# A four-layer graph network on one core: each group's aggregates turned behind the next group's first gather and scattered behind its second

## The reference, cut to what matters

```python
vdeg = jnp.maximum(H_pruned.sum(axis=1), EPS)
edeg = jnp.maximum(H_pruned.sum(axis=0), EPS)
dv_isqrt = 1.0 / jnp.sqrt(vdeg)
de_inv = 1.0 / edeg
transformed = x_final @ W
agg = H_pruned.T * dv_isqrt[None, :] @ transformed
agg = agg * de_inv[:, None]
msg = dv_isqrt[:, None] * (H_pruned @ agg)
msg = msg @ Theta
return jax.nn.relu(msg)
```

## Time and profile before

| | us |
|---|---|
| median of the three timed runs | 2352.01 (2350.14 to 2352.56) |
| the profiled execution's own device time | 2343.1 |
| its span, first to last instruction | 2341.3 |
| PE busy in it | 2045.4 (87%) |
| DVE busy | 1727.1 (74%) |
| ACT busy | 754.1 (32%) |
| mean granted TensorE clock | 0.944 |

### The profile page before, as it was taken

One profiled execution on the slowest core, in us unless ns is written; L12 is line 12 of the kernel. 1 busy time (PEld: TensorE's weight loads), 2 busy tenths in 40 slices (PEclk: granted clock), 3 DMA queues, 4 the chain that ended last, 5 costly groups with the idle time before them and its releaser, 6 DMA issues. The chain is left out here.

```text
span 2341.3 us, 35832 instructions
## 1 busy us (share of the span) xinstructions
PE 2045.4 (87%) x15658; PEld 721.4 (31%) x15658; DVE 1727.1 (74%) x2056; ACT 754.1 (32%) x869; POOL 4.5 (0%) x18
## 2 busy tenths in 40 slices
PE   7998998899977777799999989987777689997997
PEld 2233333223221211233444323221111134333333
DVE  5998923288889999855541358879999965555998
ACT  0000000076634433201110036644344311112897
POOL 0000000000000000000000000000000000000000
PEclk9999999999988888799999999998888889998999
DMA  9984999899659999977789989929999987776994
GB/s 372 421 342 183 411 429 427 370 406 373 249 220 402 428 430 430 401 262 270 265 312 406 428 369 382 375 89 370 424 429 431 425 325 269 273 288 239 350 418 180
DMA packets 128043, 812.13 MB, mean 347 GB/s; under 512 B 8336, under 2 KB 10384, under 8 KB 76432
## 3 DMA queue, kind: packets, MB, share of 16 engines
q1 hardware_dynamic: 125840, 808.51, 85.9%
q10 hardware_dynamic: 2048, 1.35, 0.2%
HBM read 673.52 MB, written 136.31 MB: 346 GB/s over the span
## 5 line engine op out<-in xcount | busy, mean ns | idle before, releaser
L1215 ACT ACTIVATE stream<-stream,negmax 128x4096 f32<-128x4096 f32 x128 | 475.1, 3711 | 482.3 <-DVE negmax L1210 482.3
L1170 PE MATMUL ps<-edgeT,node_twice 64*128 64x512 f32 x1024 | 283.1, 673 | 156.8 <-DVE mx L1205 156.7
L1205 DVE CUSTOM_DVE_ANT_0 stream<-ps,stream 128x1024 f32<-128x1024 f32 x280 | 330.5, 1219 | 30.5 <-PE ps L1170 26.5
L1170 PE MATMUL ps<-edgeT,query_twice 64*128 64x512 f32 x1024 | 248.1, 616 | 4.3 <-DVE mx L1205 2.7
L579 PE MATMUL ps<-stream,moved_block 128*64 128x512 f32 x960 | 216.6, 600 | 23.6 <-DMA stream<-in_adj 23.6
L1716 PE MATMUL ps<-stream,xw 32*64 32x512 f32 x4096 | 226.5, 589 | 1.8 <-issue 1.2
L1170 PEld LDWEIGHTS ps<-edgeT,node_twice 64*128 64x128 f32 x1024 | 94.3, 201 | 343.2 <-DVE mx L1205 242.3
L1188 PE MATMUL ps<-stream,ones 128*1 128x512 f32 x1024 | 173.3, 811 | 9.4 <-DVE stream L1760 9.4
L1249 ACT ACTIVATE query_twice<-ps,less_one_exponent 128x512 int32<-128x512 int32 x256 | 154.9, 688 | 14.8 <-PE ps L1339 12.4
L1832 DVE STREAM_TRANSPOSE stream<-spare 128x4096 f32<-128x4096 f32 x22 | 97.5, 4433 | 72.5 <-PE ps L1716 51.8
L1800 ACT COPY moved_block<-ps 128x512 f32<-128x512 f32 x16 | 9.4, 586 | 408.2 <-PE ps L1688 408.2
(11 more groups left out here) (233 smaller groups left out, 1961.5 us busy)
## 6 DMA issues: line engine op xcount, KB each, us to landing
stream<-in_adj SPq DMA_DIRECT2D x118, 2048.0 KB, 16.9
pruned<-stream SPq DMA_DIRECT2D x64, 2048.0 KB, 14.7
stream<-in_adjT SPq DMA_DIRECT2D x63, 2048.0 KB, 12.0
moved_block<-in_adj SPq DMA_DIRECT2D x24, 2048.0 KB, 13.4
spare<-pruned SPq DMA_DIRECT2D x22, 2048.0 KB, 11.5
query_twice<-pruned SPq DMA_DIRECT2D x22, 2048.0 KB, 11.5
node_twice<-pruned SPq DMA_DIRECT2D x20, 2048.0 KB, 11.2
spare<-in_adj SPq DMA_DIRECT2D x18, 2048.0 KB, 9.7
```

What stands on the lines that cost most here:

```text
L1170: last = nc.tensor.matmul(ps[:, 2 * slot + h, :], stationary[F * h:F * h + F, rows_n], bank_of(edgeT[F * h:F * h + F, :], c), start=True, ...
L1205: nc.vector.tensor_tensor_reduce(out=out[:, cols], in0=ps[:, 2 * slot:2 * slot + 2, :].rearrange("p a b -> p (a b)"), in1=block_in[:, cols ...
L1215: nc.scalar.activation(out, out, ACT.Exp, bias=negmax[:, s:s + 1], accum_out=zsum[:, s:s + 1]).then_inc(exp_done, 1)
```

## The change

It moves two calls in PE's order. aggregate(g-1), which stood at the end of group g-1, now stands behind gather(4g); scatter(g-1), which stood behind gather(4g), now stands behind gather(4g+1). aggregate(7) and scatter(7) stay at the end. No instruction, wait or buffer is added or taken away, and the programs of the other engines stay as they are.

```diff
                 for g in range(groups):
                     for c in range(CH):
                         gather(CH * g + c)
                         if c == 0 and g > 0:
+                            aggregate(g - 1)
+                        if c == 1 and g > 0:
                             scatter(g - 1)
                     if g == 0:
                         pe.wait_ge(inverse_ready, 1)
...
                         last.then_inc(copies_ready, 1)
-                    aggregate(g)
+                aggregate(groups - 1)
                 scatter(groups - 1)
```

## The result

The changed kernel takes 2357.09 us (median of 11 runs, 2352.63 to 2360.15) against 2349.81 us before (11 runs, 2347.07 to 2352.56): a ratio of 1.0026, 95% interval 1.0018 to 1.0035. It is slower, by 6 to 7 us (the two medians are 7.3 apart, the ratio comes from all runs and gives 6.1); the forecast was slower by 12.5.

A forecast was written before the change was run, and what follows sets the result against it. PE sets the period before; after, a ring through turn and load binds. Per pass, start +4.6 or +4.5, ring +5.1, end -3.4, together +12.5 us on the 2352.01 median: 2364.5 us, range 2353.8 to 2371.6.

The forecast's parts named there:

- the ring: From scatter's end through turn, load and gather to the next scatter's end: 31.48 us per period, +0.85, +5.1 per pass.
- What bounds the kernel, and what hides it: PE sets the 30.63 us period; its only wait is for ACT's copy; load 12 is only 0.3 us ahead.
- The copy's wait: Aggregate waits for ACT's copy of gathered sums, some 0.8 us per group; a gather now covers it in seven of eight.
- The start: Up to the end of scatter(0), gather(4) and gather(5) now come first: +4.6 us in the first pass, +4.5 in the second.
- The end: Between scatter(6) and scatter(7) one gather less stands: 10.07 us instead of 13.51, a gain of 3.4 us per pass.
- Sum and base: Passes of +6.3 and +6.2 us give +12.5, passed on in full; on the timed median 2352.01 that is 2364.5.
- The load in time: Rival: the load behind a scatter is there 7.5 us after issue; -6.2 us in all, 2345.8; 6% to a gain.
- The clock: Rival: PE's clock falls at each wait in the ring, 1.75 us more for each of 14 gathers, 2389 us; 6%.

The follow-up runs named there:

- the doubled turn: DVE turns the third chunk of each group twice: 2349.37 us in the order before, 2441.63 us in the changed order, single runs.
- the split: Turn of chunk 4g+2 and load of chunk 4g+5 cut into halves: changed order 2343.25 us, ratio 0.9968; order before 2350.25 us, 1.0000.
- late loads: In the second pass the last layer's loads wait for the last scatter to end: order before 2348.69 us, changed order 2355.38 us.

## Why the prediction was half right

The mechanism was right and the size wrong. The step that failed is the term of the ring, +5.1 us for the six periods of each pass: it measured +2.3 and +3.5. Everything else in the sum came within about 1.5 us.

- **What bounds the kernel, and what hides it.** Right. PE's only wait in a period was the copy's, and the load was 0.3 us behind it in cover. The run with aggregate alone shows how little that cover was: 2.2 us of wait for the load instead of 0.7 for the copy.
- **The copy's wait costs 0.7 per period, and covering it is worth nothing in the ring.** Right: with it (scatter alone moved) 1.0027, without it 1.0025.
- **The ring: period 31.48, up 0.85, +5.1 per pass.** Right in kind, shown by the doubled turn and by the split; too large in size. In the three profiles it was 31.27 on average, and before it was not 30.63 but 30.89 in the first pass and 30.68 in the second. Two things made the term too large. The sum took DVE's start behind the issue, 9.09, and added 0.12 until PE starts; over the twelve loads of the first profile after, PE started 9.04 behind the issue (8.86 to 9.17), so the sum had 0.17 too much in each period, 2.0 us in all. And the other side of the difference was one clean period times six, where the row of the first to the last scatter would have given 185.3 and 183.9 for six: the pauses of PE inside scatters, in the trace of before for anyone who adds up the periods, cost before 1.9 us in the two passes, and in the changed kernel they don't show, for a reason that stays open. 10.2 us were forecast for the two middles. The shorter ring takes 2.5 off (12 x 0.21, of which the 2.0), the pauses of before 1.9, and 5.8 are left.
- **The start, +4.6 and +4.5.** Right in the second pass (+4.4). In the first, +4.5 from gather(2) on in the first pair of profiles; the table's 5.5 holds also that gather(0) stands differently to load 2 from run to run.
- **The end, -3.4 each.** Right up to the start of the last scatter, which stands 13.5 us behind the end of the one before it in every profile of before and 10.1 in every one of the changed kernel, and right with late loads (3.4). The table differs by what the last scatter loses. In the first pass it is 14.3 to 15.2 us long in the changed kernel and 14.0 to 14.3 before, so -2.9. In the second it lost 2.3 us in the profile that I worked from and 4.3 and 4.6 in the other two, where the clock fell behind the pause, against 2.1 to 2.4 in the changed kernel, so -4.9.
- **Sum and base.** Nothing shows that what follows takes up the shift: the stage is longer by 7.9 us and the timed kernel by 6 to 7. The profiled execution, 8.9 us below the median, should have been a warning: one execution was the source for a difference of 12 us, and its last scatter was the shortest of the three.
- **The rivals.** The load in time: no, in the first profile DVE could start on it 8.8 to 9.2 us behind its issue. The clock: no; behind each of the 36 waits in three profiles, 1.14 to 1.74 us, the gather took 3.58 or 3.59 us. One window:

```profile
1061.07:1064.65 3.58, 3.58 (x17) 1.05 (x17) 3.58 (x1) 1.25 (x7) 0.00 (x0) 1.00 1.05 399
```

But it decides two of the experiments, where PE waits about 2.3 and 5.8 us, at the price that the rival named, 1.7 us and more for each gather. And it cost the kernel before 1.7 us in two of its three profiles, behind a pause.

## What to carry to other kernels

Before a call is moved past another in a hand-written order, follow what the moved call gives back (here a buffer) through all engines to the call that it is now behind; if that chain ends in the moved call's own next turn, the sum of its links is a lower bound of the period (here 31.3 us, where PE's own work is 29.9), and the wait that the move removes may be inside it. Take the difference of two whole stretches, not of one clean period times their number, and use more than one profiled execution when the effect is under half a percent. If a ring through a load binds, cutting the turn and the load in halves can open it without another buffer.

## What the runs showed of the hardware

- **The order of small matmuls decides how many run at once.** 256 matmuls with 32 rows and 64 output partitions each, about 0.59 us long, take 13.92 us when four products go to the lower 64 output partitions and the next four to the upper, and 26.0 us when 64 products in a row go to the same half. The Trainium skill, page "TensorE: Matmul & The Clock Gate", section "The mechanism", has matmuls on different tiles of the array run at the same time. The trace agrees: 256 times 0.59 us is 151 us of matmuls in 13.92. Whether a product here waits for its part of the array or for its place in PSUM, no run separates, since both come again together.
- **Behind some waits of PE the clock falls, behind others it holds.** It held behind all 36 waits of 1.14 to 1.74 us in the three profiles of the changed kernel, at 1.00, 2.4 GHz. Behind twelve waits of 2.17 to 2.39 us, with aggregate alone moved, it fell eight times (a gather of 5.28 us at 0.68) and held four times (3.58), so the length of the wait alone doesn't say which. Behind twelve of 5.7 to 5.9 us it fell each time (5.75 us at 0.62 in the window shown). The Trainium skill, page "TensorE: Matmul & The Clock Gate", section "HAM oscillation", tells of a kernel that lost the full clock at a DMA wait of 3 to 5 us in every turn of its loop; the doubled turn is such a case and agrees, and the waits near 2.3 us are shorter and still lost it eight times.
- **Loads beside PE can stop it.** PE paused 2.1 to 2.9 us in a scatter that ran beside three loads of 2048 KB, in the three profiles of either kernel, and not at all, in either order, when these were held back. That it waits for code, and that the pauses of 0.7 us in the first pass are the same thing, is likely, not shown.
- **Half a load is not half as late.** 1024 KB landed 5.5 us behind its issue and the second half, issued 1.1 us later, after 7.1, against 9.0 for the 2048 KB in one.
